# Loading the adjacency matrix in two transfers of 1024-column runs for every two pieces

## What is computed

```
h = max(layernorm(x), 0);  x = x + L0(h, adj)    # (a*adj + (1-a)*I) rows scaled by 1/sum, @ h, @ W.T + b, relu
h = max(layernorm(x), 0);  x = x + L1(h, adj)    # hyperbolic: adj @ (gamma * XW), adj @ (gamma - 1), row sums
h = max(layernorm(x), 0);  x = x + L2(h, adj)    # max of (h @ W.T + b) over the rows of the 32 largest adj entries
h = max(layernorm(x), 0);  x = x + L3(h, adj)    # (adj + I) scaled by degrees, @ x, @ W + b
```

## Time and profile before

| | |
|---|---|
| median of 3 runs | 4870.3 us (4865.9 to 4888.2) |
| the profiled execution: its own time, and its span | 4907.8 us, 4905.8 us |
| adjacency pass: first and last copy of a pair (L755) | 92.8 us, 1516.5 us |
| mean granted clock of PE over the span | 0.856 of full speed |

### The profile page before, as it was taken

How to read it: one execution, slowest core, us unless ns; L and a number is a source line. 1 busy time by engine, 2 the same in 40 slices (tenths; PEclk the granted TensorE clock), 3 DMA queues, 4 the chain that set the end, 5 groups by cost and what they waited for, 6 DMA issues and landing times.

```text
span 4905.8 us, 75402 instructions
## 1 busy us (share of the span) xinstructions
PE 3704.8 (76%) x29572; PEld 3587.6 (73%) x29572; DVE 1942.5 (40%) x4119; ACT 1618.2 (33%) x3264; POOL 2570.8 (52%) x2363
## 2 busy tenths in 40 slices
PE   4999999999999994947649471276777777777783
PEld 4999999999999994936649470266666667666683
DVE  5677778778784210221112212122222222222224
ACT  3777877777774320210202102110110101010125
POOL 2998989898993005252341533644444454444410
PEclk9999999999999996968869685577887778787797
DMA  4999999999998884836547471255555555555571
GB/s 149 394 386 363 388 359 382 362 377 363 386 379 317 292 293 134 279 126 227 197 145 267 140 237 59 83 203 184 206 200 188 195 186 200 194 198 189 194 246 44
DMA packets 569428, 1191.04 MB, mean 243 GB/s; under 512 B 45182, under 2 KB 87103, under 8 KB 569087
## 3 DMA queue, kind: packets, MB, share of 16 engines
q1 hardware_dynamic: 490672, 1082.67, 61.1%
q0 software_dynamic: 42368, 86.85, 6.0%
q10 hardware_dynamic: 36046, 16.82, 1.2%
HBM read 905.12 MB, written 281.05 MB: 242 GB/s over the span
## 4 chain that ended last, share of the span: by engine, by line
PE 69%; issue 21%; DVE 5%; ACT 3%; DMA 1%; POOL 1%; SPq 0%; ACTq 0%; DVEq 0%; another core or an unknown queue 0%
PE psT L698 18%; PE psU L572 16%; PE psT L655 15%; PE psT L560 7%; PE psU L698 6%; PE psU L655 5%; DVE D L1302 1%; ACT junk_rows L842 1%; DMA adj_turned<-ATS 1%; POOL D L467 1%; PE psT L695 0%; PE psY L624 0%; ACT D L762 0%; ACT ATS L755 0%; SPq L364 0%
## 5 line engine op out<-in xcount | busy, mean ns | idle before, releaser
L475 POOL DMA_INDIRECT D<-h_table,idx_now x1324 | 1257.6, 950 | 1838.7 <-DVE idx_now L1366 1164.4
L467 POOL TENSOR_TENSOR D<-D,iota 128x512 f32<-128x512 f32 x1024 | 1309.5, 1308 | 118.3 <-ACT D L762 103.0
L698 PE MATMUL psT<-ATS,PIECES 128*128 128x129 f32 x6144 | 979.3, 306 | 411.8 <-issue 392.3
L698 PEld LDWEIGHTS psT<-ATS,PIECES 128*128 128x128 f32 x6144 | 883.6, 219 | 472.8 <-issue 457.1
L655 PE MATMUL psT<-GR,PIECES 128*128 128x129 f32 x6144 | 837.1, 282 | 330.5 <-issue 325.7
L572 PE MATMUL psU<-HB,ATS 128*128 128x129 f32 x8192 | 1009.6, 277 | 32.8 <-ACT ATS L755 28.9
L655 PEld LDWEIGHTS psT<-GR,PIECES 128*128 128x128 f32 x6144 | 775.2, 198 | 350.2 <-issue 350.0
L572 PEld LDWEIGHTS psU<-HB,ATS 128*128 128x128 f32 x8192 | 962.0, 193 | 40.0 <-ACT ATS L755 33.5
L1302 DVE MAX8 D<-D 128x8 f32<-128x512 f32 x1024 | 646.2, 683 | 318.9 <-POOL D L467 311.9
L755 ACT ACTIVATE ATS<-psT 128x1024 f32<-128x1024 f32 x512 | 524.5, 1024 | 312.7 <-PE psT L560 218.4
L1528 DVE TENSOR_TENSOR GR<-psT,GR 128x387 f32<-128x387 f32 x240 | 123.5, 556 | 1155.6 <-PE psU L698 922.9
(11 more groups left out here) (335 smaller groups left out, 1882.1 us busy)
## 6 DMA issues: line engine op xcount, KB each, us to landing
PIECES<-adj_turned SPq DMA_DIRECT2D x512, 1024.0 KB
PIECES<-in_adj SPq DMA_DIRECT2D x256, 1024.0 KB
adj_turned<-ATS SPq DMA_DIRECT2D x512, 512.0 KB, 8.1
D<-h_table,idx_now POOLq DMA_INDIRECT x1324
h_table<-HB ACTq DMA_DIRECT2D x8, 512.0 KB
base_rows<-ATS ACTq DMA_DIRECT2D x64, 64.0 KB
D<-base_rows ACTq DMA_DIRECT2D x64, 64.0 KB
D<-h_table ACTq DMA_DIRECT2D x64, 64.0 KB
```

The lines of the kernel that those rows point to most:

```text
L467: pool.tensor_tensor(key, key, iota[:, :], ALU.mult).then_inc(keyed, 1)
L475: pool.indirect_dma_start((near_ring if done is near_gathered else ring)[par][:, slot, :], None, near_table if done is near_gathered else ...
L698: last = nc.tensor.matmul(acc(m % 2, r), wide[q % SLOTS][:, b, r * P:(r + 1) * P], Hc[c % 2][:, jj, :], start=(jj == 0 and opens(r)), stop ...
```

## The change

Two neighbouring pieces (n and n + 1, n even) now share one area of SBUF, a **double** with runs of 1024 columns; there are two such areas in the room of the four slots. A piece is a view of half a double, so its row tiles lie 1024 columns apart instead of 512. SP loads a double with two transfers, each of two row tiles, 128 x 2 x 1024 (1 MB, runs of 4 KB). SP goes through the pieces two at a time: four stores, then the waits for both old pieces, then the two transfers. Either transfer carries rows of both pieces, so PE, ACT and DVE wait for both before they read either piece.

```diff
-    adj_v = adj.rearrange("(g r p) (c x) -> g c p r x", p=P, r=TPG, x=PIECE)
+    adj_v = adj.rearrange("(g r p) (c x) -> g c p r x", p=P, r=TPG, x=2 * PIECE)
...
-        pieces = [PIECES[:, i * TPG * PIECE:(i + 1) * TPG * PIECE].rearrange("p (r x) -> p r x", r=TPG)
-                  for i in range(SLOTS)]
+        doubles = [PIECES[:, i * TPG * 2 * PIECE:(i + 1) * TPG * 2 * PIECE].rearrange("p (r x) -> p r x", r=TPG)
+                   for i in range(SLOTS // 2)]
+        pieces = [doubles[i // 2][:, :, i % 2 * PIECE:(i % 2 + 1) * PIECE] for i in range(SLOTS)]
...
-            for n in range(NPIECES):
+            for n in range(0, NPIECES, 2):
+                for old in (n - SLOTS, n - SLOTS + 1):
+                    if old >= 0:
+                        store_pairs(old)
                 if n >= SLOTS:
-                    store_pairs(n - SLOTS)
-                    sp.wait_ge(pair_transposed, 2 * (n - SLOTS + 1))
-                    sp.wait_ge(masked, 2 * (n - SLOTS + 1))
+                    sp.wait_ge(pair_transposed, 2 * (n - SLOTS + 2))
+                    sp.wait_ge(masked, 2 * (n - SLOTS + 2))
                     if (n - SLOTS) % NPC == 0:
                         sp.wait_ge(scanned, 2 * (n - SLOTS) + 1)
-                sp.dma_start(pieces[n % SLOTS], adj_v[n // NPC, n % NPC, :, :, :]).then_inc(piece_loaded[n % SLOTS], 16)
+                for h in range(2):
+                    rows = slice(2 * h, 2 * h + 2)
+                    sp.dma_start(doubles[n // 2 % 2][:, rows, :], adj_v[n // NPC, n % NPC // 2, :, rows, :])\
+                        .then_inc(piece_loaded[n % SLOTS + h], 16)
...
-                    pe.wait_ge(piece_loaded[n % SLOTS], 16 * (n // SLOTS + 1))
+                    for half in (n % SLOTS // 2 * 2, n % SLOTS // 2 * 2 + 1):
+                        pe.wait_ge(piece_loaded[half], 16 * (n // SLOTS + 1))
```

More of the change, by code:

```diff
@@ L758, in mask @@
                 n, rows = K // 2, slice(K % 2 * KROWS, (K % 2 + 1) * KROWS)
-                act.wait_ge(piece_loaded[n % SLOTS], 16 * (n // SLOTS + 1))
+                for half in (n % SLOTS // 2 * 2, n % SLOTS // 2 * 2 + 1):
+                    act.wait_ge(piece_loaded[half], 16 * (n // SLOTS + 1))
                 if n >= NKEY:
@@ L1294, in adjacency_pass @@
                                     prep = prepare(first, end)
-                        dve.wait_ge(piece_loaded[n % SLOTS], 16 * (n // SLOTS + 1))
+                        for half in (n % SLOTS // 2 * 2, n % SLOTS // 2 * 2 + 1):
+                            dve.wait_ge(piece_loaded[half], 16 * (n // SLOTS + 1))
                         pk.mark(v.tensor_scalar(zero, pieces[n % SLOTS][:, :, 0:PREFIX], 0.0, None, ALU.is_equal))
```

## The result

| | kernel before | changed kernel |
|---|---|---|
| median of 4 runs | 4870.5 us (4865.9 to 4888.2) | 4926.1 us (4921.2 to 4933.8) |
| profiled execution, its span | 4907.8, 4905.8 | 4930.1, 4928.2 |
| adjacency pass, first to last copy of a pair | 92.8 to 1516.5: 1423.7 us | 91.8 to 1566.8: 1475.0 us |

The ratio of the runs is 1.0104, with a 95% interval of 1.0085 to 1.0123: 56 us slower at the medians. The forecast was no measurable difference, 4867 us, in a range up to 4896; the time lies outside it.

What follows compares the result with a forecast made beforehand. PE was taken to bound the adjacency pass. The shorter wait for `scanned` gave -3 us and all other terms 0: 4907.8 - 3 = 4904.8 us profiled, a median of 4867 us, range 4846 to 4896.

Steps and rivals of the forecast that it cites:

- the bound for a transfer's landing: Adjacency pass: a double's two transfers land 7.5 us after issue (bounds 6.7 and 9.2), within 10.1 us, costing PE 0 us.

Runs made afterwards that it cites:

- e4: The kernel before with each piece's load, still one at a time, asked for one piece later: 0 us difference (0.9985 to 1.0007), adjacency pass 1427.7 us.
- f2: The changed kernel with stores of the turned pairs cut to an eighth (128 of 1024 columns), results wrong: adjacency pass 1430.3 us, only the pass counts.

## What to carry to other kernels

A queue with a few per cent to spare was not idle enough for bursts here: what counts is how long the last byte of the largest batch takes beside all other traffic, against the time from its release to its use. When two buffers are merged, the number of places halves and the lead shrinks, here from 15.4 to 10.1 us; look for room for one more half before looking for longer runs. And take the bound for a transfer's landing from rows inside the stage it will run in, with that stage's backlog added, never from a quiet stretch alone.

## What was new about the chip

- With loads in bursts of two beside stores DMA moved 376 GB/s over 242 us at a DMA share of 1.01 (341 over 8 us of one double), against 387 to 391 at 1.01 to 1.02 where single loads and stores took turns. With hardly any stores it reached 418 to 422 in stretches of 2 us. Neither POOL's work nor the distance of the rows in DRAM (closed blocks against rows 32 KB apart) made a difference.
- Holding one load back at a group's start and then sending two 1.5 to 2.7 us apart left stores late for some 40 us after it (the kernel before, from 280.83 to 317.27 in group 2). With each load asked for one piece later, and without that hold, ACT's wait for stores fell from 62.8 to 1.0 us at no cost (e4).
- Loads alone moved 420 GB/s with runs of 4 KB and 390 with runs of 2 KB (from 24 to 28 of the changed kernel and of the kernel before).
- A load in an emptied queue started slowly also with runs of 4 KB: 110 GB/s in the stretch from 112 to 114 of f2, whose double was issued at 111.19.
